# Splitting activations in two halves in the second attention: the subtraction moves from VectorE to GpSimd

## The reference, cut to what matters

```python
qkv = jnp.einsum('bsd,ed->bse', x, Wqkv)
q, k, v = jnp.split(qkv, 3, axis=-1)
logits = jnp.einsum('bihd,bjhd->bhij', q, k) * scale + pos_bias[None]
attn = jax.nn.softmax(logits, axis=-1)
out = jnp.einsum('bhij,bjhd->bihd', attn, v).reshape(B, S, D)
return jnp.einsum('bsd,ed->bse', out, Wout)
```

## Time and profile before

| | us |
|---|---|
| median of 3 runs | 2237.12 (2235.95 to 2242.12) |
| the profiled execution | 2235.95, of it the span 2234.3 |
| busy over the span: PE, PEld | 1764.3 (79%), 1101.2 (49%) |
| DVE, ACT, POOL | 1122.0 (50%), 1024.8 (46%), 1012.5 (45%) |
| second attention: GpSimd bias adds | 192 x 2.375 = 452.1 busy |
| second attention: VectorE score pass | 512 x 0.714 = 340.4 busy, and 512 x 0.140 |
| second attention: low parts on VectorE | 64 x 0.69 |

### The profile page before, as it was taken

How to read it: one execution, slowest core, us unless ns; L and a number is a source line. 1 busy time by engine, 2 the same in 40 slices (tenths; PEclk the granted TensorE clock), 3 DMA queues, 4 the chain that set the end, 5 groups by cost and what they waited for, 6 DMA issues and landing times. The chain is left out here.

```text
span 2234.3 us, 33907 instructions
## 1 busy us (share of the span) xinstructions
PE 1764.3 (79%) x10759; PEld 1101.2 (49%) x10759; DVE 1122.0 (50%) x2399; ACT 1024.8 (46%) x1356; POOL 1012.5 (45%) x778
## 2 busy tenths in 40 slices
PE   3888889870599999999999638887887888747933
PEld 2455555540387787787787523333433433235510
DVE  3666666537513313313313148878787787437211
ACT  1455555543313322222223117877787788813400
POOL 3344444320234344343333407777777677724212
PEclk8899999985799999999999858989998999869965
DMA  3333333306201101101100253222222222043999
GB/s 102 87 96 94 94 104 91 94 11 202 84 1 47 47 0 47 47 0 47 45 2 28 77 174 86 67 71 80 80 66 71 81 65 59 10 173 137 345 318 330
DMA packets 129732, 204.38 MB, mean 91 GB/s; under 512 B 14303, under 2 KB 84063, under 8 KB 129668
## 3 DMA queue, kind: packets, MB, share of 16 engines
q1 hardware_dynamic: 107896, 163.40, 24.6%
q10 hardware_dynamic: 16096, 20.65, 2.6%
q0 software_dynamic: 5680, 19.57, 2.2%
HBM read 95.96 MB, written 56.69 MB: 68 GB/s over the span
## 5 line engine op out<-in xcount | busy, mean ns | idle before, releaser
L761 POOL TENSOR_TENSOR l_prob<-l_prob,l_bias 128x1024 f32<-128x1024 f32 x192 | 452.1, 2375 | 149.2 <-ACT l_prob L865 148.4
L1315 POOL TENSOR_TENSOR f_hl<-f_full,f_hh 128x512 fp32r<-128x512 f32 x192 | 247.6, 1290 | 439.9 <-DVE f_hh L1357 283.2
L922 DVE CUSTOM_DVE_ANT_0 l_slot<-l_slot,l_bias 128x512 f32<-128x512 f32 x512 | 340.4, 714 | 52.8 <-PE l_slot L999 51.7
L1357 DVE CAST f_hh<-f_full 128x512 fp32r<-128x512 f32 x128 | 74.8, 585 | 397.7 <-ACT f_full L1336 396.2
L868 ACT ACTIVATE l_prob<-l_prob 128x1024 f32<-128x1024 f32 x256 | 271.1, 1071 | 0.0
L1401 PE MATMUL f_ps<-f_hh,f_hi_h 128*128 128x512 f32 x1024 | 267.1, 397 | 0.0
L1411 PE MATMUL f_ps<-f_hl,f_hi_h 128*128 128x512 f32 x1024 | 265.8, 396 | 0.0
L429 DVE TENSOR_REDUCE l_peak<-l_slot 128x2 f32<-128x256 f32 (+3 forms) x256 | 206.2, 821 | 111.3 <-PE l_slot L526 109.0
L1336 ACT ACTIVATE f_full<-f_ps,f_h_s 128x512 f32<-128x512 f32 x128 | 86.3, 687 | 332.6 <-PE f_ps L1411 308.9
L372 ACT ACTIVATE l_prob<-l_slot 128x1024 f32<-128x1024 f32 (+3 forms) x256 | 174.7, 706 | 96.3 <-PE l_slot L545 93.4
L1401 PEld LDWEIGHTS f_ps<-f_hh,f_hi_h 128*128 128x128 f32 x1024 | 192.8, 188 | 49.3 <-ACT f_hh L1329 2.7
(11 more groups left out here) (209 smaller groups left out, 2691.5 us busy)
## 6 DMA issues: line engine op xcount, KB each, us to landing
l_stacks<-l_parts SPq DMA_DIRECT2D x384, 128.0 KB, 2.7
inter<-e_stage POOLq DMA_DIRECT2D x32, 512.0 KB, 5.1
c_rows<-inter SPq DMA_DIRECT2D x32, 512.0 KB, 9.6
attn<-l_out_sb ACTq DMA_DIRECT2D x16, 512.0 KB, 2.8
f_raw<-in_L_ffn_h_w SPq DMA_DIRECT2D x16, 512.0 KB, 4.2
e_w<-in_L_ffn_f SPq DMA_DIRECT2D x32, 256.0 KB, 4.4
l_bias<-ext ACTq DMA_DIRECT2D x16, 448.0 KB, 11.8
l_x_in<-in_L_attn_x SPq DMA_DIRECT2D x8, 512.0 KB, 3.8
```

The lines of the kernel that those rows point to most:

```text
L761: return eng.tensor_tensor(probs(n), src, bias[:, h:h + 2, j * P:j * P + T], ALU.add)
L922: ins = dve.tensor_tensor_reduce(src, src, bias[:, 4 * g + 2 * pr + a, t * P:t * P + T], 1.0, 3 * NEG, ALU.add, ALU.max, peak[:, g, a, pr, ...
L1315: pool.tensor_tensor(hl[layer % 2][:, o], full[:, n % 2], hh[layer % 2][:, o].bitcast(F32), ALU.subtract).then_inc(h_lo.sem, 1)
```

## The change

The second attention takes the form of the first. Three fp32 buffers in SBUF, `x_full`, `qk_full` and `mix_full` (128x1024 each), are new. For each piece ScalarE now copies the bank `single` to a half of such a buffer, without rounding, and this copy is the last read of the bank. When both halves of a pair are there, VectorE rounds the pair with one 128x1024 copy in SBUF (`x_high`, `qk_high`, `mix_high`) and GpSimd subtracts with one 128x1024 instruction (`x_low`, `qk_low`, `mix_low`). For a sequence that is 8 subtractions on VectorE less, 4 copies on VectorE more, 4 subtractions on GpSimd more; ScalarE has as many instructions as before. The rounding and the subtraction stand at the step of the pair's second piece: 19, 23, 27 and 29. GpSimd's subtraction stands ahead of that step's bias add, and behind those of all steps before. The DMAs that save `xh` and `xl` and those that fill `stacks` wait for GpSimd's subtraction in place of VectorE's. ScalarE's third q/k copy of a sequence waits until the first pair is subtracted.

```diff
+        x_full, qk_full, mix_full = (sb(f"{n}_full", [P, 2, T]) for n in ("x", "qk", "mix"))
...
-                           (18, ("x_turn", 1, 0)), (19, ("x_turn", 1, 1)), (22, ("qk", 1, 0)), (23, ("qk", 1, 1)),
-                           (24, ("mix_turn", -1, 0)), (27, ("mix_turn", -1, 1)), (28, ("qk", 1, 2)), (29, ("qk", 1, 3)),
-                           (31, ("out", -1, 0), ("store", -1, 0))):
+                           (18, ("x_turn", 1, 0), ("x_copy", 1, 0)), (19, ("x_turn", 1, 1), ("x_copy", 1, 1)),
+                           (19, ("x_high", 1, 0), ("x_low", 1, 0)),
+                           (22, ("qk", 1, 0), ("qk_copy", 1, 0)), (23, ("qk", 1, 1), ("qk_copy", 1, 1)),
+                           (23, ("qk_high", 1, 0), ("qk_low", 1, 0)),
+                           (28, ("qk", 1, 2), ("qk_copy", 1, 2)), (29, ("qk", 1, 3), ("qk_copy", 1, 3)),
+                           (29, ("qk_high", 1, 1), ("qk_low", 1, 1)),
+                           (24, ("mix_turn", -1, 0), ("mix_copy", -1, 0)), (27, ("mix_turn", -1, 1), ("mix_copy", -1, 1)),
+                           (27, ("mix_high", -1, 0), ("mix_low", -1, 0)), (31, ("out", -1, 0), ("store", -1, 0))):
...
-                     "maxima": tops_ready, "x_turn": xl_ready, "qk": low_ready, "heads_turn": mix_ready, "mix_turn": ml_ready}
+                     "maxima": tops_ready, "x_turn": xt_full, "qk": qk_copied, "heads_turn": mix_ready, "mix_turn": mt_full}
...
-                    if kind == "x_turn" and n == KD - 1:
+                    if kind == "x_low":
                         wait(sp, xn_ready, TT, b)
                         sp.dma_start(xn_d[b], xn[:]).then_inc(xn_saved.sem, 16)
-                        wait(sp, xh_ready, KD, b)
+                        wait(sp, xh_ready, 1, b)
...
-                        hold(sp, held_sp, low_ready, n // 2 * 2 + 2, b)
+                        hold(sp, held_sp, low_ready, n // 2 + 1, b)
...
+                    if kind == "x_low":
+                        wait(pool, xh_ready, 1, b)
+                        pool.tensor_tensor(xl[:], x_full[:], xh[:].bitcast(F32), ALU.subtract).then_inc(xl_ready.sem, 1)
+                    if kind == "qk_low":
+                        wait(pool, high_ready, n + 1, b)
+                        pool.tensor_tensor(parts[:, n, 0:4:3], qk_full[:], parts[:, n, 1:3].bitcast(F32),
+                                           ALU.subtract).then_inc(low_ready.sem, 1)
+                    if kind == "mix_low":
+                        wait(pool, mh_ready, 1, b)
+                        pool.tensor_tensor(mixt[:, 1], mix_full[:], mixt[:, 0].bitcast(F32), ALU.subtract)\
+                            .then_inc(ml_ready.sem, 1)
...
-                    if kind == "qk":
+                    if kind == "qk_copy":
                         wait(act, qk_ps, n + 1, b)
-                        if n % 2 == 0:
-                            for g in (n, n + 1):
-                                wait(act, stack_in[g], 6, b - 1)
-                        act.copy(parts[:, n // 2, 1 + n % 2], single[:]).then_inc(high_ready.sem, 1)
+                        if n == 2:
+                            wait(act, low_ready, 1, b)
+                        act.copy(qk_full[:, n % 2], single[:]).then_inc(qk_copied.sem, 1)
...
-                    if kind == "x_turn":
-                        wait(dve, xh_ready, n + 1, b)
-                        dve.tensor_tensor(xl[:, n], single[:], xh[:, n].bitcast(F32), ALU.subtract).then_inc(xl_ready.sem, 1)
-                    if kind == "qk":
-                        wait(dve, high_ready, n + 1, b)
-                        dve.tensor_tensor(parts[:, n // 2, n % 2 * 3], single[:], parts[:, n // 2, 1 + n % 2].bitcast(F32),
-                                          ALU.subtract).then_inc(low_ready.sem, 1)
...
+                    if kind == "x_high":
+                        wait(dve, x_saved, 2, b - 1)
+                        wait(dve, xt_full, KD, b)
+                        dve.tensor_copy(xh[:], x_full[:]).then_inc(xh_ready.sem, 1)
+                    if kind == "qk_high":
+                        for g in (2 * n, 2 * n + 1):
+                            wait(dve, stack_in[g], 6, b - 1)
+                        wait(dve, qk_copied, 2 * n + 2, b)
+                        dve.tensor_copy(parts[:, n, 1:3], qk_full[:]).then_inc(high_ready.sem, 1)
+                    if kind == "mix_high":
+                        wait(dve, mt_full, KD, b)
+                        dve.tensor_copy(mixt[:, 0], mix_full[:]).then_inc(mh_ready.sem, 1)
```

More of the change, by code:

```diff
@@ L645, in biased_attention @@
         eps_done, rstd_ready = sem("eps_done", 1), sem("rstd_ready", 1)
-        xt_ps, xh_ready, xl_ready = sem("xt_ps", KD), sem("xh_ready", KD), sem("xl_ready", KD)
+        xt_ps, xt_full = sem("xt_ps", KD), sem("xt_full", KD)
+        xh_ready, xl_ready = sem("xh_ready", 1), sem("xl_ready", 1)
         v_ps, v_ready = sem("v_ps", 1), sem("v_ready", 1)
-        qk_ps, high_ready, low_ready = sem("qk_ps", 4), sem("high_ready", 4), sem("low_ready", 4)
+        qk_ps, qk_copied = sem("qk_ps", 4), sem("qk_copied", 4)
+        high_ready, low_ready = sem("high_ready", 2), sem("low_ready", 2)
         stack_in = [sem(f"stack_in{g}", 6, unit=16) for g in range(QUADS)]
@@ L843, in emit @@
                                            scale=rstd[:, t:t + 1]).then_inc(xn_ready.sem, 1)
-                    if kind == "x_turn":
+                    if kind == "x_copy":
                         wait(act, xt_ps, n + 1, b)
                         if n == 0:
-                            wait(act, x_saved, 2, b - 1)
-                        act.copy(xh[:, n], single[:]).then_inc(xh_ready.sem, 1)
-                    if kind == "qk":
+                            wait(act, xl_ready, 1, b - 1)
+                        act.copy(x_full[:, n], single[:]).then_inc(xt_full.sem, 1)
+                    if kind == "qk_copy":
                         wait(act, qk_ps, n + 1, b)
-                        if n % 2 == 0:
-                            for g in (n, n + 1):
-                                wait(act, stack_in[g], 6, b - 1)
-                        act.copy(parts[:, n // 2, 1 + n % 2], single[:]).then_inc(high_ready.sem, 1)
+                        if n == 2:
+                            wait(act, low_ready, 1, b)
+                        act.copy(qk_full[:, n % 2], single[:]).then_inc(qk_copied.sem, 1)
                     if kind == "v":
@@ L872, in emit @@
                         act.copy(o_sb[:, n % 2], o_bank[:, ::-1]).then_inc(o_copied.sem, 1)
-                    if kind == "mix_turn":
+                    if kind == "mix_copy":
                         wait(act, mt_ps, n + 1, b)
-                        act.copy(mixt[:, 0, n], single[:]).then_inc(mh_ready.sem, 1)
+                        if n == 0:
+                            wait(act, ml_ready, 1, b - 1)
+                        act.copy(mix_full[:, n], single[:]).then_inc(mt_full.sem, 1)
                     if kind == "out":
@@ L903, in emit @@
                            .then_inc(shift_ready.sem, 1)
-                    if kind == "x_turn":
-                        wait(dve, xh_ready, n + 1, b)
-                        dve.tensor_tensor(xl[:, n], single[:], xh[:, n].bitcast(F32), ALU.subtract).then_inc(xl_ready.sem, 1)
-                    if kind == "qk":
-                        wait(dve, high_ready, n + 1, b)
-                        dve.tensor_tensor(parts[:, n // 2, n % 2 * 3], single[:], parts[:, n // 2, 1 + n % 2].bitcast(F32),
-                                          ALU.subtract).then_inc(low_ready.sem, 1)
-                    if kind == "mix_turn":
-                        wait(dve, mh_ready, n + 1, b)
-                        dve.tensor_tensor(mixt[:, 1, n], single[:], mixt[:, 0, n].bitcast(F32), ALU.subtract)\
-                           .then_inc(ml_ready.sem, 1)
+                    if kind == "x_high":
[10 more added lines that the diff above has]
+                        dve.tensor_copy(mixt[:, 0], mix_full[:]).then_inc(mh_ready.sem, 1)
                     if kind == "score":
@@ L980, in emit @@
                         weight, cut = (wk if n % 2 else wq), slice(n // 2 * P, (n // 2 + 1) * P)
-                        wait(pe, xl_ready, KD, b)
+                        wait(pe, xl_ready, 1, b)
                         product(single[:], [(weight[:, p, k, cut], (xl if q else xh)[:, k]) for k in range(KD)
@@ L1045, in emit @@
                         out = claim_pair(kind, n, i)
-                        wait(pe, ml_ready, KD, b)
+                        wait(pe, ml_ready, 1, b)
                         for t in range(TT):
```

5 lines of the change are left out of this document (3 added, 2 removed).

## The result

The changed kernel takes 2264.55 us (median of 4 runs, 2264.38 to 2276.08) beside 2239.62 us for the kernel before: a ratio of 1.0117 with a 95% interval of 1.0081 to 1.0153. Two more runs of the changed kernel, of 2257.59 and 2269.11 us, count in the ratio, which is not exactly that of the medians. The medians differ by 25 us, where 14.7 were forecast. The time lies in the stated range of 2234 to 2266, by 1.5 us, but above the forecast's own range of 2243 to 2259. The way and most of the mechanism are as forecast; one term of the sum is less than half of what it should be.

A forecast was written before the change was run, and what follows sets the result against it. No engine was full; engines waiting in fixed order set the turn, its end hanging on VectorE's fourth bias add. 7 x 1.5 + 4.2 = +14.7 us on 2235.95 gave 2250.7, 2251.8 on the median's scale, stated as 2251; range 2234 to 2266.

The forecast's parts named there:

- the forecast's own range: Whole kernel: 2243 to 2259 us, from a term of +0.4 to +2.6 a turn; chance 0.48.
- The place: Second attention: a turn's end hangs on when VectorE starts the fourth bias add, which frees a slot TensorE awaits.
- The stall: VectorE's SBUF roundings wait for GpSimd's running instruction, ending 0.54 us after it; each costs 0.69 to 0.69 + 2.375 us.
- The walk: Place-by-place passage through a second-attention turn with GpSimd's subtractions put in, estimating when each of the four roundings ends.
- The bias add: Fourth bias add of a turn, behind the second `qk_high`: late by 1.5 us, bounds -0.4 to +1.8.
- +1.5 a turn: Second `qk_high` delays the fourth bias add, lengthening each turn by 1.5 us; TensorE's wait grows from 1.63 to about 3.1.
- `out` and the next turn follow: Turn's end: nothing hides the fourth bias add's 1.5 us delay, so output and next turn come later.
- The clock: A turn can also lose in TensorE's clock after longer waits; named for the range of +0.4 to +2.6 a turn.
- The number of turns: The +1.5 us counted once in each of the 7 turns (0 to 6) that prepare a sequence.
- Head and tail: Bare chains at the second attention's ends: first score +2.6 us, last `out` about +1.6, together +4.2.
- The first: Rival: TensorE's bank waits of 2.6 us a turn go, roundings mostly meet a free port; 2223 us, chance 0.14.
- The third: Rival: GpSimd becomes the bound; second `qk_high` waits for two instructions, +3.9 a turn, 2267 us, chance 0.12.

The follow-up runs named there:

- experiment 1: Changed kernel with rounding and subtraction of the second q/k pair at step 30 in place of 29; 2238.27 us, ratio 0.9996 to the kernel before.
- 4: Kernel before plus an unread VectorE maximum over 1792 columns, about 1.9 us, right ahead of the fourth bias add; 2266.43 us, ratio 1.0134.
- 5: Kernel before plus an unread VectorE maximum over 832 columns, about 0.95 us, ahead of the fourth bias add; 2253.20 us, ratio 1.0052.
- 6: Changed kernel plus 12 unread TensorE filler matmuls at step 30, in the wait for the fourth bias add; 2249.94 us, ratio 1.0042 to the kernel before.
- experiment 2: Changed kernel, but VectorE rounds each of the 8 pieces from the PSUM bank, not pairs in SBUF; 2251.03 us, ratio 1.0065 to the kernel before.
- 7: Kernel before plus 5 unread TensorE filler matmuls in its 1.63 us wait at step 30; 2240.31 us, ratio 0.9995.

## Why the prediction was right, and where its size was off

- *The place.* The prediction put the decision at the start of the fourth bias add. Experiments 1, 4 and 5 show it: take the stall from there and the loss is gone; put a delay there and the turn grows by more than the delay.
- *The stall.* It was read off a 1.50-us rounding in another stage and a 0.81-us instruction, for an instruction that the second attention did not have. The walk had 1.4 us for `x_high` from ready to end, 1.9 for the first `qk_high`, 0.7 to 3.1 for `mix_high`, 2.7 for the second `qk_high`; measured are 1.53, 1.84, 2.86 and 2.47.
- *The bias add* was forecast 1.5 us late; it is 27.44 - 25.67 = 1.77 late, near the upper bound of 1.8.
- *The mis-sized term* is "+1.5 a turn". Measured: +3.2 in each of five turns. The step that fails is the one from the bias add to the turn's end, "`out` and the next turn follow", taken one to one. Another 3.04 - 1.77 = 1.27 us go into TensorE's matmuls behind the longer wait, and 6 shows that the turn's loss goes with them. The clock was named, but only as a reason for a wide range of 0.4 to 2.6 a turn, and the measured term is outside that too. A row at hand warned of it: the output took 3.86 us at 1459.71, behind a wait of 1.63, where it takes 3.08 at full clock (experiments 1 and 6). It did not give the price: experiments 2 and 7 have that output at full clock and turns as long as before. So the size could have been bounded better, but hardly read off.
- *The number of turns.* Seven were counted at one price. Turn 0 has no output and lost 1.2. The sum is 4.1 + 1.2 + 16.1 + 4.1; of the last term 3.0 stand up to the output copy of turn 6, and 1.2 in turn 7 and the tail.
- *Head and tail:* +3.0 up to the first score for +2.6, and another 1.1 up to the second statistics, for which the sum had nothing. The last output waits 3.91 - 1.49 = 2.4 us more, and turn 7 with the tail is 1.2 longer, for +1.6.
- *Rivals.* The first (faster, by up to 2.6 a turn) described a gain that may be there: with the stall out of the way (experiment 1) turns are 1.9 us shorter than before. But in that kernel nothing of the second q/k pair stands ahead of the fourth bias add any more, which comes 0.9 us earlier, and the output runs at full clock. The kernel before with its last subtraction behind that bias add was not run, so how much the bank gives is open. The third gives 2267, near the measured 2264.6, but its mechanism isn't what happened: the rounding waited for one GpSimd instruction, not two, and ScalarE's exponentials waited 2.2 us for GpSimd in the whole stage.
- *Luck.* The time is inside the range only because the range took in half of that third rival. The direction and the place were reasoned; that 2264.6 is under 2266 was not.

## What to carry to other kernels

Before work goes from VectorE to GpSimd, look at what is left on VectorE: a copy or cast from SBUF to SBUF that met a busy GpSimd ended 0.55 us after GpSimd's running instruction here, up to 2.87 us for one of 0.69, and it belongs where nothing that frees a slot is queued behind it. A delay on the chain to TensorE is to be priced at more than its own length if TensorE stands still meanwhile; compare the duration of the same matmuls behind a short and behind a long wait, and then time whole turns, since a slow stretch can come back elsewhere (experiments 2 and 7). Where a chain runs bare, as at the head and tail of a pipeline, it pays to try the faster engine there, even if the other has the work in the steady part.

## What was not expected of the hardware

- The price of an idle TensorE. A delay of 0.93 us cost 2.1 us in a turn and one of 1.93 cost 3.4; 3.0 us of matmuls without use in a wait of 3.35 us won 3.1 us back.
- A filler of 1.43 to 1.45 us in a shorter wait won 1.3 us in its stretch and nothing in the turn; value products at 1.93 us turned up 3.4 us behind the start of the output copy. In experiment 2 the same wait of 1.63 us was followed by outputs of 3.08 us and of up to 4.17.
- The wait between VectorE and GpSimd goes both ways: two queued bias adds took 5.12 us with a rounding between them, 4.70 without.
